# The closing stage of a two-layer macaron block: tail parts of the intermediate in products of 112 rows, turns at other tiles, squares summed on GpSimd, the HGRN result taken in halves

## The chip, the cores and the metric

The kernel runs on one core of a Trainium2 chip. A core has TensorE (PE; its weight loads, PEld, are shown apart), VectorE (DVE), ScalarE (ACT), GpSimd (POOL) and SyncE (SP), each with an instruction queue of its own, and 16 DMA engines. The metric is the time of one execution on the device, in microseconds (us). Of the kernel before there are three runs with a median of 2899.85 us.

## The reference, cut to what matters

The input is 16 sequences of 256 tokens with 256 features (4096 rows of 256). Two layers follow each other. The first (a mixture of experts, an attention, the same experts again) is not touched. The second is computed in the closing stage:

```python
    x = x + 0.5 * _L1_ffn_ref(_layernorm(x, axis=-1), L1_ffn_lut, L1_ffn_gate_idx, L1_ffn_up_idx, L1_ffn_down_idx)
    x = x + _L1_attn_ref(_layernorm(x, axis=-1), L1_attn_Wi, L1_attn_Wf, L1_attn_Wg, L1_attn_Wo, L1_attn_gnorm_w)
    x = x + 0.5 * _L1_ffn_ref(_layernorm(x, axis=-1), L1_ffn_lut, L1_ffn_gate_idx, L1_ffn_up_idx, L1_ffn_down_idx)
```

with, in `_L1_ffn_ref` (256 features, 688 in the intermediate, weights looked up in a table of 16 values),

```python
        gate = _ghost_linear(x, gate_idx, lut)
        up = _ghost_linear(x, up_idx, lut)
        h = jax.nn.silu(gate) * up
        return _ghost_linear(h, down_idx, lut)
```

and, in `_L1_attn_ref` (HGRN, a gated linear recurrence along the 256 tokens),

```python
        gate = jax.nn.sigmoid(f)
        v = jax.nn.silu(i) * (1.0 - gate)
        ...
        _, o = jax.lax.associative_scan(combine, (gate, v), axis=1)
        rms = o * jax.lax.rsqrt(jnp.mean(o * o, axis=-1, keepdims=True) + EPS)
        o = rms * gnorm_w * g * jax.nn.sigmoid(g)
        return jnp.einsum('btd,hd->bth', o, Wo)
```

## The kernel before, in words

The whole kernel is one launch with stages that follow each other: router, experts, attention, router, experts, and `closing`, which runs from about 2262 us to the end.

`closing` works on 8 units of 512 rows (four groups of 128, two sequences). A unit passes three stages: IN (first feed-forward), MID (HGRN) and OUT (second feed-forward). The loop over `i` goes through 10 rounds; round `i` has unit `i` in IN, `i-1` in MID and `i-2` in OUT, so rounds 2 to 7 have all three, round 0 only IN, round 1 IN and MID, round 8 MID and OUT, round 9 only OUT. The order on each engine is written out by hand in one block per engine, and semaphores join them; each engine works its list strictly in order.

TensorE's list in a full round (L1883 on): the six gate/up tiles of IN (`gate_up`, tiles 0 to 5), with the turn (transposition, `turn`) of unit `i-2` for OUT behind tile 1 and that of unit `i-1` for MID behind tile 3; the three HGRN projections f, i, g (`project`); `down` of IN; the turn of unit `i+1` for IN; the six gate/up tiles of OUT, with the sums of squares (`sums`) behind tile 3; `mix` (the product with the HGRN output weights); `down` of OUT. Products are made in three: each operand is split into a high and a low part, and high x high, high x low and low x high are added (`split_matmul`, L1433 to L1435).

The intermediate's 688 features are five tiles of 128 and a tail of 48 (tile 5). `UP_AT` is 64: a product of 112 columns makes the gate of the tail in rows 0 to 47 and its up part in rows 64 to 111 of one PSUM bank. ScalarE takes silu of the gate (`f_sil`, L1589), VectorE multiplies with up (`gated`, `f_hs`, L1680), ScalarE rounds the result to its high part (`high`, `f_hT`, L1594) and VectorE makes the low part (`low`, `f_hT`, L1686). `down` then does for each of four groups of 128 tokens 6 x 3 products, the last three of them over the 48 rows 64 to 111.

Banks: `pair[0]` and `pair[1]`, two banks each, are taken in turn by gate/up tiles and projections; `psT` (two banks) takes the turned tiles, which ScalarE reads as the high part (`f_lnT`, L1584) and VectorE as the low part (`f_lnT`, L1669); `psY` (two banks) takes `down` and `mix`. The sums of squares are written to four columns of `pair[1][0]`, from which VectorE makes `f_ms` (L1735) and GpSimd `f_orstd` (L1559). `mixed` (L1743) adds the HGRN result to the residual (`f_x`), for four groups in a row; moments (L1653, L1656), GpSimd's `norm` (L1539, L1541) and `normalise` (`f_ln`, L1663) prepare the next stage. GpSimd also adds the two halves of the input, `f_x` and `f_xb` (L1533).

## Time and profile before

| | us |
|---|---|
| median of 3 runs | 2899.85 (2894.0 to 2900.19) |
| the profiled execution | 2890.84 |
| its span, first to last instruction | 2889.1 |
| TensorE busy in it (mean granted clock 0.930) | 2472.3 (86%) |
| VectorE, ScalarE, GpSimd busy | 1782.9, 894.5, 1224.7 |

The page cuts the span into 40 slices of 72 us. The closing stage is the last nine of them. A digit is the busy share in tenths, and PEclk is the clock that TensorE was granted (9 is 90% or more of full speed):

```profile
PE   6455489999999999999999999956576489999997
PEld 5344378888888888888888888845454377777776
DVE  5332257787777777777777777745222266666543
ACT  6222223333333333333333333325322133333321
POOL 2277634545455545554555445421588221111110
PEclk9588889999999999999999999965789799999999
```

Two things in reading the order in time: a product's length is modelled to the end of its way through the array, so products overlap, and what counts is the distance from start to start; and "idle before" is counted from the modelled end of the instruction before.

### The profile page before, as it was taken

To read this page: it belongs to the slowest core of one execution; us is meant where nothing else is said; L and a number is where in the kernel's file an instruction comes from. 1 tells how busy PE (TensorE), PEld (TensorE's weight loads), DVE (VectorE), ACT (ScalarE), POOL (GpSimd) and SP (SyncE) were. 2 spreads that over 40 slices of the span, in tenths; PEclk is the share of its full clock that TensorE was granted. 3 is DMA by queue.
4 is the path that set the end of the run, shared out by engine and by line. 5 is a ranking of instruction groups with operands and counts; after the bars stand their busy time and mean duration, and the time that the engine had idled before them with its cause. 6 is when DMAs were issued, how large, how long until landed. Compare 5 with 4: busy or idle time off the path is not lost. (4 is left out here: it accounts for less than half of the span.)

```text
span 2889.1 us, 44938 instructions
## 1 busy us (share of the span) xinstructions
PE 2472.3 (86%) x17054; PEld 2122.6 (73%) x17054; DVE 1782.9 (62%) x3522; ACT 894.5 (31%) x1885; POOL 1224.7 (42%) x1193
## 2 busy tenths in 40 slices
PE   6455489999999999999999999956576489999997
PEld 5344378888888888888888888845454377777776
DVE  5332257787777777777777777745222266666543
ACT  6222223333333333333333333325322133333321
POOL 2277634545455545554555445421588221111110
PEclk9588889999999999999999999965789799999999
DMA  6699700000000000000000000014899210000000
GB/s 218 172 247 241 149 21 17 7 16 20 20 5 16 19 19 5 16 19 19 5 16 19 20 5 17 10 40 131 228 216 198 52 30 23 22 23 15 8 8 15
DMA packets 192917, 169.48 MB, mean 59 GB/s; under 512 B 28513, under 2 KB 185153, under 8 KB 192193
## 3 DMA queue, kind: packets, MB, share of 16 engines
q1 hardware_dynamic: 163472, 117.05, 13.7%
q0 software_dynamic: 24576, 37.77, 7.1%
q10 hardware_dynamic: 4656, 11.80, 1.3%
q8 instruction: 138, 2.26, 0.3%
q14 instruction: 75, 0.61, 0.1%
HBM read 117.88 MB, written 53.13 MB: 59 GB/s over the span
## 5 line engine op out<-in xcount | busy, mean ns | idle before, releaser
L947 POOL TENSOR_TENSOR a_orstd<-a_ms,minus_half 128x8 f32<-128x8 f32 x64 | 106.2, 1660 | 638.1 <-DVE a_ms L1107 638.1
L1080 DVE TENSOR_TENSOR a_at<-a_psB,causal 128x384 f32<-128x384 f32 x512 | 260.4, 550 | 101.6 <-PE a_psB L1252 101.6
L927 POOL TENSOR_SCALAR a_pick<-a_index,lut_row 128x258 f32<-128x258 int32 x240 | 278.9, 1162 | 24.4
L1100 DVE RECIPROCAL a_rz<-a_rz 128x256 f32<-128x256 f32 x128 | 221.5, 1732 | 0.0
L635 PE MATMUL e_psX<-ident,e_xg 128*128 128x128 f32 x256 | 62.7, 332 | 171.6 <-DMA e_xg<-rows,slot_tok 170.7
L759 DVE TENSOR_TENSOR e_hT<-e_psH,e_sil 128x128 f32<-128x128 f32 x128 | 37.3, 291 | 268.3 <-ACT e_sil L716 147.5
L635 PEld LDWEIGHTS e_psX<-ident,e_xg 128*128 128x128 f32 x256 | 32.6, 160 | 214.4 <-DMA e_xg<-rows,slot_tok 209.7
L930 POOL TENSOR_TENSOR a_found<-a_found,a_pick 128x258 f32<-128x258 f32 x240 | 177.5, 739 | 20.0
L1313 PE MATMUL a_psD<-a_v,a_at 128*128 128x128 f32 x1536 | 181.8, 275 | 0.0
L1313 PEld LDWEIGHTS a_psD<-a_v,a_at 128*128 128x128 f32 x1536 | 176.9, 192 | 0.1
L1680 DVE TENSOR_TENSOR f_hs<-f_pair,f_sil 128x512 f32<-128x512 f32 x96 | 66.2, 691 | 168.5 <-PE f_pair L1435 150.5
L606 POOL DMA_INDIRECT e_xg<-rows,slot_tok x128 | 128.0, 1000 | 91.1 <-POOLq L73 52.7
L1433 PE MATMUL f_pair<-f_lnT,wguT 128*128 128x512 f32 (+1 forms) x352 | 144.3, 410 | 18.2 <-DVE f_ms L1735 10.2
L1433 PE MATMUL a_psA<-wo_high,a_oT 128*128 128x256 f32 x512 | 151.9, 297 | 1.5 <-DVE a_oT L1060 1.5
L1028 ACT ACTIVATE a_sq<-a_psD 128x512 f32<-128x512 f32 x128 | 76.5, 598 | 240.5 <-PE a_psD L1313 227.7
L1434 PE MATMUL a_psA<-wo_low,a_oT 128*128 128x256 f32 x512 | 145.0, 283 | 0.0
L1435 PE MATMUL a_psA<-wo_high,a_oT 128*128 128x256 f32 x512 | 144.9, 283 | 0.0
L1435 PE MATMUL f_pair<-f_lnT,wguT 128*128 128x512 f32 (+1 forms) x352 | 140.2, 398 | 0.0
L1434 PE MATMUL f_pair<-f_lnT,wguT 128*128 128x512 f32 (+1 forms) x352 | 139.9, 397 | 0.0
L1589 ACT ACTIVATE f_sil<-f_pair 128x512 f32<-128x512 f32 x96 | 57.2, 597 | 260.4 <-PE f_pair L1435 260.4
L1433 PE MATMUL f_psY<-wdT,f_hT 128*128 128x256 f32 (+1 forms) x384 | 122.1, 318 | 14.5 <-DVE f_x L1743 7.6
L952 POOL TENSOR_TENSOR a_o<-a_o,a_orstd 128x512 f32<-128x512 f32 x128 | 131.0, 1044 | 5.0
(243 smaller groups left out, 7516.1 us busy)
## 6 DMA issues: line engine op xcount, KB each, us to landing
e_wg<-in_L_ffn_w_gate SPq DMA_DIRECT2D x128, 128.0 KB
e_wu<-in_L_ffn_w_up SPq DMA_DIRECT2D x128, 128.0 KB
e_wd<-in_L_ffn_w_down SPq DMA_DIRECT2D x128, 128.0 KB
rows<-r_row SPq DMA_DIRECT2D x32, 320.0 KB, 3.1
stream_b<-r_zeros SPq DMA_DIRECT2D x11, 384.0 KB, 6.2
stream_c<-rows SPq DMA_DIRECT2D x33, 128.0 KB, 3.2
r_xt<-in_L_attn_hidden_states SPq DMA_DIRECT2D x16, 256.0 KB, 3.9
stream_a<-r_xt SPq DMA_DIRECT2D x16, 256.0 KB, 4.9
```

The source lines that it names most:

```text
L606: pool.indirect_dma_start(out=xg[:, e % U, :], out_offset=None, in_=rows, in_offset=bass.IndirectOffsetOnAxis(ap=slot_tok[:, e:e + 1], axi ...
L635: nc.tensor.transpose(psX[u][:, c, :], xg[:, e % U, c * P:(c + 1) * P], cst["ident"][:, :]).then_inc(turned[u], 1)
L927: nc.gpsimd.tensor_scalar(pick[:, :, :], index[:, :, :], float(c), w["lut"][:, c:c + 1], ALU.is_equal, ALU.mult).then_inc(picked, 1)
L930: nc.gpsimd.tensor_tensor(out=found[:, :, :], in0=found[:, :, :], in1=pick[:, :, :], op=ALU.add).then_inc(looked, 1)
L947: nc.gpsimd.tensor_tensor(out=flat(orstd[:, :, :]), in0=ms[:, :], in1=cst["minus_half"][:, 0:TT * HQ], op=ALU.pow).then_inc(orstd_ok, 1)
L952: nc.gpsimd.tensor_tensor(out=part, in0=part, in1=orstd[:, :, 2 * a:2 * a + 2].unsqueeze(3).to_broadcast([P, TT, 2, DV]), op=ALU.mult).the ...
L1080: nc.vector.tensor_tensor(out=at[:, h, :], in0=psB[h % 2][:, 0:3 * P], in1=cst["causal"][:, :, :].rearrange("p a i -> p (a i)"), op=ALU.mu ...
L1100: nc.vector.reciprocal(rz[:, a, :], rz[:, a, :]).then_inc(rz_ok, 1)
L1313: mm = nc.tensor.matmul(psD[:, t, h * DV:(h + 1) * DV], bt[:, h, i * P:(i + 1) * P], v[:, n % 2, j, h * DV:(h + 1) * DV], start=(j == 0), ...
L1433: nc.tensor.matmul(out, lhs[0], rhs[0], start=first, stop=False)
L1434: nc.tensor.matmul(out, lhs[0], rhs[1], start=False, stop=False)
L1435: return nc.tensor.matmul(out, lhs[1], rhs[0], start=False, stop=last)
```

## The change

It touches `closing`, one weight group and one load of the expert stage before it.

1. The tail of the intermediate. `high` writes the tail's high part to rows 0 to 47 of `hT[:, 0, 5]`, `low` its low part to rows 64 to 111 of the same; rows 32 to 63 are zeroed once by ScalarE. The weights' tail lies in rows 0 to 47 and again in 64 to 111 (`down_groups`, and one more load of 64 columns). `down` makes two products of 112 rows for each group of tokens, against the weights' high and low part, where it made three of 48 rows (the product low x low comes with it). `down` also waits at its start for the low parts of the first five tiles alone, and for the tail's ahead of the first 112-row product.
2. The turns of OUT and MID come behind tiles 0 and 2 of IN, not 1 and 3; the moments of the next unit behind tile 3, not 4.
3. The squares of the two halves of features are added by GpSimd (`sum_of_squares`), the sums take 4 calls, not 8 (the trace has two records for a product of plain f32, so 16 for a unit before), and go to `psT[0]`, not `pair[1][0]`. The OUT tiles take the two pairs strictly in turn, and the last of them doesn't wait for `ms_ok`.
4. `mixed` is done in two halves, the low part of tile 5 between them, and `down` of OUT waits for each half apart.
5. The first unit's load comes in halves, and VectorE adds it (`add_first`), not GpSimd.

```diff
-    tail = [w_dn[:, c, INTER - UP_AT - FLAST:INTER] for c in range(DC)]
-    groups.append((wdT[UP_AT:UP_AT + FLAST, 0, FT - 1, :], wdT[UP_AT:UP_AT + FLAST, 1, FT - 1, :], tail, UP_AT))
+    tail = [w_dn[:, c, UPS:UPS + UP_AT + FLAST] for c in range(DC)]
+    groups.append((wdT[0:UP_AT + FLAST, 0, FT - 1, :], wdT[0:UP_AT + FLAST, 1, FT - 1, :], tail, 0))
...
-            return (f if stage == IN else 9 + f + (f >= 4)) % 2
+            return (f if stage == IN else 1 + f) % 2
...
+                def load_first():
+                    for k in range(2):
+                        half = slice(2 * k, 2 * k + 2)
+                        sp.dma_start(xb[:, half, :], sv[1][0][:, half, :]).then_inc(x_first[k], 16)
+                        sp.dma_start(x1[:, 0, half, :], sv[0][0][:, half, :]).then_inc(x_first[k], 16)
...
+                def sum_of_squares(m):
+                    pool.wait_ge(osq_ok, DC * m + DC)
+                    nc.gpsimd.tensor_tensor(out=osq[:, 0, :], in0=osq[:, 0, :], in1=osq[:, 1, :], op=ALU.add).then_inc(osum_ok, 1)
...
+                nc.scalar.activation(hT[32:UP_AT, 0, FT - 1, :].rearrange("p (g t) -> p g t", t=P),
+                                     cst["ident"][32:UP_AT, :].unsqueeze(1).to_broadcast([UP_AT - 32, G, P]), ACT.Copy,
+                                     scale=0.0).then_inc(tail_zero, 1)
...
-                        if f == 4 and i + 1 < U:
+                        if f == 3 and i + 1 < U:
                             moments_of(IN, i + 1)
...
+                    if mid is not None:
+                        mixed(mid, 0)
                     if last is not None:
                         low(OUT, last, FT - 1)
                     if mid is not None:
-                        mixed(mid)
+                        mixed(mid, 1)
...
-                def down(stage, m):
-                    pe.wait_ge(h_lo[stage], FT * m + FT)
-                    for k in range(2):
...
+                def down(stage, m, k):
+                    pe.wait_ge(h_lo[stage], FT * m + FT - 1)
+                    for g in (2 * k, 2 * k + 1):
+                        dst = psY[k][:, (g % 2) * D:(g % 2 + 1) * D]
+                        for f in range(FT - 1):
+                            split_matmul(nc, dst, [hT[:, part, f, g * P:(g + 1) * P] for part in range(2)],
+                                         [wdT[:, part, f, :] for part in range(2)], f == 0, False)
+                        if g == 0:
+                            pe.wait_ge(h_lo[stage], FT * m + FT)
+                            pe.wait_ge(tail_zero, 1)
+                        for part in range(2):
+                            mm = nc.tensor.matmul(dst, hT[0:UP_AT + FLAST, 0, FT - 1, g * P:(g + 1) * P],
+                                                  wdT[0:UP_AT + FLAST, part, FT - 1, :], start=False, stop=(part == 1))
+                    mm.then_inc(down_ps[stage], 1)
...
-                    pe.wait_ge(osq_ok, DC * m + DC)
+                    pe.wait_ge(osum_ok, m + 1)
+                    psT_free(m)
...
-                        if f == 1 and last is not None:
-                            turn(OUT, last)
-                        if f == 3 and mid is not None:
-                            turn(MID, mid)
+                        if f == 0 and last is not None:
+                            turn(OUT, last, mids)
+                        if f == 2 and mid is not None:
+                            turn(MID, mid, mids)
...
-                            pe.wait_ge(res_ok[MID], G * mid + G)
+                                pe.wait_ge(res_ok[MID], G * mid + 2 * k + 2)
```

`psT_free` makes TensorE wait until VectorE has read all earlier turned tiles (`lnT_lo`) and earlier sums (`ms_ok`).

How the lists move. VectorE in a full round, from the two results `f_y` of the unit that is done, through the IN tiles, before:

```order
L1700 SCALAR_TENSOR_TENSOR f_y<-f_psY,f_x 128x512 x2
L1680 TENSOR_TENSOR f_hs<-f_pair,f_sil 128x512
L1686 TENSOR_TENSOR f_hT<-f_hs,f_hT 128x512
L1680 TENSOR_TENSOR f_hs<-f_pair,f_sil 128x512
L1686 TENSOR_TENSOR f_hT<-f_hs,f_hT 128x512
L1669 TENSOR_TENSOR f_lnT<-f_psT,f_lnT 128x512 x2
L1680 TENSOR_TENSOR f_hs<-f_pair,f_sil 128x512
L1686 TENSOR_TENSOR f_hT<-f_hs,f_hT 128x512
L1680 TENSOR_TENSOR f_hs<-f_pair,f_sil 128x512
L1686 TENSOR_TENSOR f_hT<-f_hs,f_hT 128x512
L1669 TENSOR_TENSOR f_lnT<-f_psT,f_lnT 128x512 x2
L1653 BN_STATS f_bs<-f_x 128x6 x4
```

and with the change (L1669 became L1698, L1680 L1709, L1686 L1716, L1653 L1682):

```order
L1730 SCALAR_TENSOR_TENSOR f_y<-f_psY,f_x 128x512 x2
L1698 TENSOR_TENSOR f_lnT<-f_psT,f_lnT 128x512 x2
L1709 TENSOR_TENSOR f_hs<-f_pair,f_sil 128x512
L1716 TENSOR_TENSOR f_hT<-f_hs,f_hT 128x512
L1709 TENSOR_TENSOR f_hs<-f_pair,f_sil 128x512
L1716 TENSOR_TENSOR f_hT<-f_hs,f_hT 128x512
L1698 TENSOR_TENSOR f_lnT<-f_psT,f_lnT 128x512 x2
L1709 TENSOR_TENSOR f_hs<-f_pair,f_sil 128x512
L1716 TENSOR_TENSOR f_hT<-f_hs,f_hT 128x512
L1682 BN_STATS f_bs<-f_x 128x6 x4
L1685 BN_AGGR f_mv<-f_bs 128x2 x4
L1709 TENSOR_TENSOR f_hs<-f_pair,f_sil 128x512
```

The low parts of the turned tiles (`f_lnT`) stand right behind `f_y` and two gatings later, and the statistics (`f_bs`) one gating sooner.

VectorE at the end of a round, from `f_ms` to the statistics of the HGRN result, before:

```order
L1735 TENSOR_SCALAR f_ms<-f_pair 128x4
L1680 TENSOR_TENSOR f_hs<-f_pair,f_sil 48x512
L1686 TENSOR_TENSOR f_hT<-f_hs,f_hT 128x512
L1686 TENSOR_TENSOR f_hT<-f_hs,f_hT 48x512
L1743 SCALAR_TENSOR_TENSOR f_x<-f_psY,f_orstd,f_x 128x256 x4
L1653 BN_STATS f_bs<-f_x 128x6 x4
```

and with the change:

```order
L1765 TENSOR_SCALAR f_ms<-f_psT 128x4
L1709 TENSOR_TENSOR f_hs<-f_pair,f_sil 48x512
L1716 TENSOR_TENSOR f_hT<-f_hs,f_hT 128x512
L1773 SCALAR_TENSOR_TENSOR f_x<-f_psY,f_orstd,f_x 128x256 x2
L1716 TENSOR_TENSOR f_hT<-f_hs,f_hT 48x512
L1773 SCALAR_TENSOR_TENSOR f_x<-f_psY,f_orstd,f_x 128x256 x2
L1682 BN_STATS f_bs<-f_x 128x6 x4
```

The four `f_x` are now two and two, with the 48-row low part between them, and `f_ms` is read from `f_psT`.

TensorE in round 1, where there is no OUT unit: the turn for the next unit (into `f_psT`), the sums, `mix`, the first tile of round 2, before:

```order
L1811 MATMUL f_psT<-ident,f_ln 128x128 x8
L1850 MATMUL f_pair<-causal,f_osq 128x1 x8
L1859 MATMUL f_psY<-woT,f_pT 128x256 x8
L1433 MATMUL f_pair<-f_lnT,wguT 128x512
L1434 MATMUL f_pair<-f_lnT,wguT 128x512
```

and with the change:

```order
L1849 MATMUL f_psT<-ident,f_ln 128x128 x8
L1892 MATMUL f_psT<-causal,f_osq 128x1 x4
L1901 MATMUL f_psY<-woT,f_pT 128x256 x8
L1433 MATMUL f_pair<-f_lnT,wguT 128x512
L1434 MATMUL f_pair<-f_lnT,wguT 128x512
```

The sums are half as many and go to the bank into which the turn just ahead of them wrote.

## Rows read from the trace of the kernel before

**Rows 1.** Busy time by stage: start:end, us, each engine, clock, DMA share, GB/s.
```profile
2400.00:2793.00 393.00, 371.79 (x2026) 310.36 (x2026) 225.75 (x456) 115.58 (x202) 58.28 (x57) 1.00 0.06 17
2436.96:2508.43 71.47, 67.74 (x370) 56.50 (x369) 43.02 (x85) 21.71 (x38) 11.68 (x11) 1.00 0.07 23
```

**Rows 2.** Waits of TensorE, closing stage: waiter, releaser, total us, times, longest.
```profile
PE f_psT L1811 <- DVE f_ln L1663: 35.5, 2, 32.3
PE f_pair L1433 <- DVE f_lnT L1669: 17.3, 11, 2.9
PE f_pair L1433 <- DVE f_ms L1735: 10.2, 7, 1.5
PE f_psY L1433 <- DVE f_x L1743: 7.6, 7, 1.1
PE f_psY L1433 <- DVE f_hT L1686: 6.8, 2, 3.9
...
PE f_pair L1433 <- DVE f_hs L1680: 1.1, 2, 0.8
```

**Rows 3.** Order in time, TensorE, `down`: start, us, line, operation, [idle before].
```profile
2467.94 0.28 PE L1434 MATMUL f_psY<-wdT,f_hT 128*128 128x256 f32 x1
2468.06 0.28 PE L1435 MATMUL f_psY<-wdT,f_hT 128*128 128x256 f32 x1
2468.27 0.38 PE L1433 MATMUL f_psY<-wdT,f_hT 48*128 48x256 f32 x1
...
2468.81 0.39 PE L1433 MATMUL f_psY<-wdT,f_hT 128*128 128x256 f32 x1
2469.04 0.28 PE L1434 MATMUL f_psY<-wdT,f_hT 128*128 128x256 f32 x1
```

**Rows 4.** Order in time: first product of `down`, turn behind it, last `down`.
```profile
2463.86 0.28 PE L1433 MATMUL f_psY<-wdT,f_hT 128*128 128x256 f32 x1
...
2473.88 1.09 PE L1811 MATMUL f_psT<-ident,f_ln 128*128 128x128 f32 x8
...
2498.30 0.39 PE L1433 MATMUL f_psY<-wdT,f_hT 128*128 128x256 f32 x1 [1.09 <-DVE f_x L1743]
```

**Rows 5.** Order in time: a 128-column product and the 112-column one behind it.
```profile
2295.94 0.40 PE L1435 MATMUL f_pair<-f_lnT,wguT 128*128 128x512 f32 x1
2296.18 0.40 PE L1433 MATMUL f_pair<-f_lnT,wguT 128*112 128x512 f32 x1
```

**Rows 6.** Order in time: the one-column products.
```profile
2485.93 1.84 PE L1850 MATMUL f_pair<-causal,f_osq 128*128 128x1 f32 x16
```

**Rows 7.** Order in time, GpSimd: an addition in place.
```profile
2501.51 2.40 POOL L1533 TENSOR_TENSOR f_x<-f_x,f_xb 128x1024 f32<-128x1024 f32 x1
```

**Rows 8.** Order in time, TensorE: ahead of the HGRN projections.
```profile
2455.55 0.50 PE L1433 MATMUL f_pair<-f_lnT,whT 128*128 128x512 f32 x1 [1.19 <-DVE f_lnT L1669]
2455.88 0.39 PE L1434 MATMUL f_pair<-f_lnT,whT 128*128 128x512 f32 x1
```

**Rows 9.** Order in time, TensorE: the last gate/up tile.
```profile
2492.12 0.48 PE L1433 MATMUL f_pair<-f_lnT,wguT 128*112 128x512 f32 x1 [1.45 <-DVE f_ms L1735]
```

**Rows 10.** Order in time, VectorE: the two lows ahead of the last `down`.
```profile
2866.81 1.41 DVE L1686 TENSOR_TENSOR f_hT<-f_hs,f_hT 128x512 fp32r<-128x512 f32 x2
```

**Rows 11.** Order in time, all engines: first loads and first addition.
```profile
2263.03 0.50 SPq L1512 DMA_DIRECT2D f_x<-x_att  x1
...
2269.47 2.33 POOL L1533 TENSOR_TENSOR f_x<-f_x,f_xb 128x1024 f32<-128x1024 f32 x1 [15.68 <-DMA f_x<-x_att]
```

**Rows 12.** Order in time, VectorE in round 1.
```profile
2357.08 1.26 DVE L1669 TENSOR_TENSOR f_lnT<-f_psT,f_lnT 128x512 fp32r<-128x512 f32 x2
2358.64 1.38 DVE L1663 TENSOR_SCALAR f_ln<-f_x,f_mv,f_rstd 128x256 f32<-128x256 f32 x4 [0.30 <-POOL f_rstd L1541]
```

**Rows 13.** Order in time, TensorE: sums in round 1.
```profile
2355.44 1.84 PE L1850 MATMUL f_pair<-causal,f_osq 128*128 128x1 f32 x16
```

**Rows 14.** Order in time, VectorE: normalising beside GpSimd's addition.
```profile
2501.57 3.45 DVE L1663 TENSOR_SCALAR f_ln<-f_x,f_mv,f_rstd 128x256 f32<-128x256 f32 x4 [1.47 <-POOL f_rstd L1541]
```

More of the change, by code:

```diff
@@ L1801, in _, with psT_free @@
                 done_turns = [0, 0, 0]
-                def turn(stage, m):
-                    pe.wait_ge(ln_ok[stage], G * m + G)
+                def psT_free(sums):
                     for other in (IN, MID, OUT):
@@ L1807, in turn @@
                             pe.wait_ge(lnT_lo[other], DC * done_turns[other])
+                    if sums > 0:
+                        pe.wait_ge(ms_ok, sums)
+                def turn(stage, m, sums):
+                    pe.wait_ge(ln_ok[stage], G * m + G)
+                    psT_free(sums)
                     done_turns[stage] += 1
@@ L1861, in mix @@
                         mm.then_inc(out_ps, 1)
[L1863 removed]
+                turn(IN, 0, 0)
                 for i in range(U + 2):
@@ L1889, in _ @@
                             pe.wait_ge(res_ok[OUT], 2 * lasts)
-                        down(IN, first)
+                        for k in range(2):
+                            down(IN, first, k)
                     if i + 1 < U:
-                        turn(IN, i + 1)
+                        turn(IN, i + 1, mids)
                     for f in range(FT):
```

100 lines of the change are left out of this document (52 added, 48 removed).

## The prediction

> **What bounds the kernel now.** I read the page first (busy shares, the 40 slices), then the table by stage for the closing stage, then the waits of TensorE in it, then the order in time of each engine through one round. The diff touches the closing stage, from about 2262 us to the end, and one load and one weight group ahead of it. In that stage TensorE is the bound: between 2400 and 2793 us it is busy 371.79 of 393.00 us at a granted clock of 1.00 (2.4 GHz), VectorE 225.75, ScalarE 115.58, GpSimd 58.28 [rows 1]. One round, in which three units pass through their three stages, takes 71.47 us (2436.96 to 2508.43) and repeats, with VectorE busy 43.02 of it. So time goes only where TensorE's own list gets shorter, or where a wait in it goes. The waits of TensorE in the stage are short and few [rows 2]: 7 times `f_ms` (10.2 us), 7 times `f_x` (7.6), 11 times `f_lnT` ahead of a product (17.3), 2 times `f_hT` (6.8), 2 times `f_ln` (35.5, of which 32.3 is the start of the stage).
>
> **The change part by part.** All times are against the profiled execution, 2890.84 us with a span of 2889.1.
>
> *The tail of the intermediate.* A product group of `down` is 5 x 3 products of 128 rows and 3 of 48 rows. Starts of 128-row products lie 0.12 apart (2467.94, 2468.06) [rows 3]. Then the first 48-row one comes after 0.21, the next 128-row one 0.54 later (three products), and its successor after 0.23: 0.98 us for five steps that would take 0.60. So there are 0.38 us of pauses, about 0.19 for each of the two changes between 128 and 48 rows. A whole `down` takes 10.02 us in the first feed-forward (2463.86 to 2473.88) and 10.13 in the last (2498.30 to the end of the round at 2508.43) [rows 1, 4]. The change puts low under high in one operand of 112 rows and needs two products: 68 for a `down`. At 0.12 each, without the two pauses, that is 8.16 us, so 8 x 1.86 + 8 x 1.97 = 30.6 us less. Is a 112-row product followed and preceded by such a pause? No row of before has 112 rows. The nearest are, on one side, these 48-row ones, on the other the 112-column ones of `gate_up`, of which the first starts 0.24 behind a 128-column one of the same length, without a pause [rows 5]. If the pauses stay, only 64 products of 0.12 go: 7.7 us. I take 30.6, since the rows with a 112 beside a 128 are the nearer in size and show no pause, and keep 7.7 as the other end. A gain below 7.7 I exclude: products get fewer, none wider.
>
> The Trainium skill (TensorEngine Tiling (Array Packing), Key Properties), to be weighed against the pauses of 0.19 us in [rows 3] and their absence in [rows 5], says that a change of tiling mode drains TensorE, and its list of configurations has none between 64 rows and 128. By that rule a 112-row product stands in the same mode as its neighbours, and the sum is the 30.6; without the rule, by the 48-row rows alone, it would be 7.7. The trace agrees with the drain at 48 rows; no run of before shows 112.
>
> *The sum of squares.* 16 products of one column take 1.84 us to their modelled end, 1.68 of it before the next product can start [rows 5, 6]; 8 of them go, 0.84 us, for 8 units 6.7 us. The GpSimd addition stands for them: 128x1024 in place takes 2.40 us [rows 7], so half of it about 1.2. It starts when ScalarE's second square ends, some 3 us behind the scans and 16 ahead of the products, while GpSimd has nothing to do. So it costs nothing, except in the first round with a HGRN unit (below).
>
> *Turns sooner.* In each of 7 rounds TensorE waits before the HGRN projections for VectorE's second part of the turned tile, 1.19 us [rows 8]. The profile counts from the modelled end of the product before; without a wait the next starts 0.16 ahead of that end [rows 5], and behind a wait the second start comes after 0.33 us and not 0.23 (2455.55, 2455.88). So the wait is worth 1.19 + 0.26 = 1.45 us. The turn now comes one gate/up tile (12 x 0.23 = 2.78 us) earlier, and there is 2.78 + 1.39 of tiles behind it instead of 1.39. What is late next is the gating of tile 4, which the projections need as well and which the moments of the next unit now precede: gated 3 starts at the end of tile 3, and it, a low and the moments (0.7 + 0.6 + 1.85 us in this round) put gated 4 at +3.15 to +3.84, where TensorE needs it at about +4.0. So the wait goes, with 0.1 to spare. Saved: 7 x 1.45 = 10.2.
>
> *The sums in another bank.* TensorE's last tile of the output feed-forward waits for `f_ms`, 1.45 + 0.26 = 1.71 us [rows 9]. With the sums in `psT[0]` that tile waits only for a gating done long before. 7 x 1.71 = 12.0.
>
> *HGRN result by half.* Behind `mix` the last `down` waits for `f_x`, 1.09 + 0.26 = 1.35 us [rows 4]. Now VectorE does low 4, two of the four `f_x`, low 5, and the other two. Counted from the end of tile 4 at 0: tile 5 ends at 1.4, silu and gated 5 at 2.9, low 4 at 3.6, first two `f_x` at 4.4, low 5 at 5.1; `mix` ends at 5.0, its second half is taken by 5.95. `down` needs the first two at 5.0, low 5 at 6.8 and the others at 9.1. Nothing waits: 7 x 1.35 = 9.4. The three waits together: 31.6 us.
>
> *First `down` and last.* In round 0 and in the last one it waits 3.9 and 2.9 us for `f_hT` [rows 2]. Now it needs only the first of two lows at its start (0.7 of 1.41) [rows 10], in round 0 also without the moments before gated 5, which held it 1.0: 1.7 and 0.7. The 0.8 us that tile 4 of the last round waits for `f_hs` go too, since the tile uses the other pair [rows 2]. Together 3.2.
>
> *First unit's addition on VectorE.* GpSimd's 2.33 us [rows 11] become VectorE's second half, 0.7 by the nearest row (half of two 128x512 lows in 1.41) [rows 10]: 1.6 less. Two more DMA issues may move the landing by up to 0.9 (at most 0.50 each, as the issue at 2263.03 [rows 11]); bounds 0.7 and 1.6, I take 1.6, as the same bytes are moved. ScalarE's zeroing lies in its idle 35 us. The extra load of 64 KB in the expert stage is at most 0.3 us at 220 GB/s; I take 0.
>
> *What gets worse: rounds 1 and 2.* With no third unit in round 1, the sums follow straight on a turn, and now write where that turn's result still lies. VectorE has read it at 2357.08 + 1.26 = 2358.34, and the sums started at 2355.44 [rows 12, 13]. They then end near 2359.2, `mix` near 2362.9, the last `f_x` 0.9 later than before, and with it the normalising for which the turn of round 2 waits (35.5 - 32.3 = 3.2 us before [rows 2]). And that turn stands before tile 1 now: 2.8 us of products, which filled the wait before, come behind it. +3.7 us; the wait grows from 3.2 to about 5.
>
> Sum: -30.6 - 6.7 - 31.6 - 3.2 - 1.6 + 3.7 = -70.0 us. The profiled execution would be 2890.84 - 70.0 = 2820.8. The median of the runs lies 9.0 us above the profiled one, so there it is 2899.85 - 70.0 = 2829.9, say 2830.
>
> **The rivals.** *A, the pauses stay with 112 rows:* for it, that no row shows such a product; against, the rule and the 112-column rows. 30.6 becomes 7.7: 2853. *B, the projections keep waiting, for gated 4:* for it, the 0.1 of slack and VectorE's order; against, that VectorE's blocks are short. At most the whole 10.2 stays: 2840. *C, the turn of the output stage comes before its normalising is done, in every round:* it would end on the other side. In before, the normalising ends at 2501.57 + 3.45 = 2505.02 [rows 14], 11.4 after `mix` starts (its 3.6 us and the 1.09 end at 2498.30 [rows 4]); after, TensorE reaches the turn 3.6 + 8.2 + 2.8 = 14.3 or more after it, so 3 us are to spare, where before the turn had 5.8 more. Each us beyond the 3 costs 7 us; slower than before by more than the measurement tells it would be from 13.9 us of lateness on (70.0 / 7 = 10.0, 0.9 for the border of 0.2%, and the 3), at about 2906. Against it: VectorE is idle 28 of 71 us in a round. *D, GpSimd's new addition slows VectorE:* VectorE's normalising takes 1.38 us alone (2358.64) and 3.45 beside GpSimd's 2.40 us addition (2501.57) [rows 7, 12, 14], and the new addition falls on the two products `f_pT` right behind the scans. If they are held for all 1.2 us, VectorE comes to the result of `down` just as that now ends, and at most 1.2 x 7 = 8 us come back: 2838. The Trainium skill (GPSIMD Engine Reference, Specifications) says that GpSimd shares its SBUF interface with VectorE's operations of two SBUF inputs. The trace agrees in kind with the normalising, though that has one tensor input; with the rule the addition would slow just that pair.
>
> **How the numbers follow.** My case 0.70 (own range 2812 to 2838, which also has the 9 us between profiled and median runs), A 0.12, B 0.09, D 0.04, C 0.03, and 0.02 for a change that does not remove the waits at all (2830 + 31.6 = 2862). The range reaches down for that offset, and up to A: 2812 to 2854. A difference of 0.2% (6 us) is about what a measurement of this kernel tells from none. Faster by more than that in all but C: 0.95; within it 0.02; slower 0.03.
>
> **What would show it.** Right: one `down` at 8.2 us; starts at 0.12 through its 112-row products; 8 one-column products; rounds of 71.47 - 1.86 - 1.97 - 0.84 - 4.51 = 62.3 us; no TensorE wait for `f_ms`, `f_x` or, but for the two last rounds, `f_lnT`; one wait near 5 us for `f_ln` in round 2. Wrong: gaps around the 112-row products (A); waits for `f_hs` before the projections (B); waits for `f_ln` in every round (C); longer `f_pT` operations and waits before tiles 1 to 3 of the last feed-forward (D). The forecast fails as a whole if the clock in the middle is below 1.00.

## The result, and the profile after

| | before | after |
|---|---|---|
| median of 4 runs each, us | 2900.02 (2894.0 to 2902.39) | 2823.36 (2821.51 to 2824.11) |
| ratio, 95% interval | | 0.9735 [0.9723, 0.9747] |
| the profiled execution, us | 2890.84 | 2821.51 |
| closing stage, first turn to the end of the last product | 603.2 | 535.0 |
| a full round | 71.46 | 62.0 |

The change makes the kernel 2.65% faster. Profile against profile it is 69.3 us, and 68.2 of them lie between the first turn and the last product. The medians differ by 76.7, since the profiled execution of before lay 9 us under its median and that of after 2 under. The further 7 us are in no stretch of these two traces; the runs of before spread by 8. The traces of the changed kernel and of its variants below, whose code ahead of the closing stage is the same, reach the first turn anywhere between 2273.4 and 2283.2 us, so whole runs differ by up to 10 us before the stage begins. What a step is worth is therefore read from the stage and from the length of a round.

The page of the kernel after, its span, busy times and the two rows of TensorE in 40 slices (now of 70.5 us):

```profile
span 2819.7 us, 44733 instructions
PE 2424.1 (86%) x16926; PEld 2097.4 (74%) x16926; DVE 1792.7 (64%) x3524; ACT 895.8 (32%) x1886; POOL 1233.4 (44%) x1200
...
PE   6456569999999999999999999995465568999997
...
PEclk9988889999999999999999999995589979999999
```

TensorE has 128 records fewer: 64 are products of the tail, the other 64 are the two records of each of 32 sum calls. The busy time by stage, for just over six full rounds and for one of them, answers to [rows 1]:

```profile
2389.50:2766.00 376.50, 372.00 (x2104) 324.29 (x2103) 252.31 (x488) 129.27 (x225) 74.83 (x68) 1.00 0.06 19
2427.36:2489.33 61.97, 61.97 (x355) 54.15 (x353) 44.09 (x85) 21.83 (x38) 12.99 (x12) 1.00 0.09 26
```

In a round TensorE is busy for the whole 61.97 us at a clock of 1.00: no wait is left. VectorE works 44.09 us instead of 43.02, and still has 18 to spare. The waits of TensorE in the stage, which answer to [rows 2]:

```profile
PE f_psT L1849 <- DVE f_ln L1692: 35.0, 2, 29.7
PE f_pair L1433 <- DVE f_lnT L1698: 9.2, 4, 3.0
PE f_psY L1433 <- DVE f_hT L1716: 4.3, 2, 2.2
PE f_psT L1892 <- issue: 3.0, 1, 3.0
PE f_psT L1849 <- DVE f_lnT L1698: 2.2, 1, 2.2
```

`f_ms` and `f_x` are gone, and of the 11 waits for `f_lnT` ahead of a product 4 are left, all in rounds 0, 1, 8 and 9. `f_ln` stays at two: the start of the stage (32.3 became 29.7) and round 2, where 3.2 became 5.3. One is new, 3.0 us ahead of the sums of round 1 (L1892); it has no releaser in the profile ("issue"). TensorE's list there waits in `psT_free` for VectorE's read of the turned tile. The prediction's sign, no wait for `f_lnT` "but for the two last rounds", holds for rounds 2 to 7 alone: the two waits of round 0 and of the start of round 1 (2.2 and 3.0 us) were in before as well and were left out of it.

The tail in `down`, in the order in time of TensorE; this answers to [rows 3]:

```profile
2456.26 0.28 PE L1435 MATMUL f_psY<-wdT,f_hT 128*128 128x256 f32 x1
2456.38 0.40 PE L1880 MATMUL f_psY<-wdT,f_hT 112*128 112x256 f32 x2
2456.61 0.28 PE L1433 MATMUL f_psY<-wdT,f_hT 128*128 128x256 f32 x1
2456.74 0.28 PE L1434 MATMUL f_psY<-wdT,f_hT 128*128 128x256 f32 x1
```

The two 112-row products (one row of the trace, x2) start 0.12 behind their forerunner and take 0.23 together; the next 128-row one has no pause behind them either. And the projections start straight behind the last gate/up tile, where [rows 8] had 1.19 us:

```profile
2444.15 0.39 PE L1435 MATMUL f_pair<-f_lnT,wguT 128*112 128x512 f32 x1
2444.38 0.39 PE L1433 MATMUL f_pair<-f_lnT,whT 128*128 128x512 f32 x1
```

The next table sets the saving against the prediction's terms stretch by stretch, from the starts of the HGRN projections in the two traces (2336.17 and 2329.64 in round 1, 2384.10 and 2382.38 in round 2, 2741.41 and 2692.40 in round 7, 2800.61 and 2742.87 in round 8; ends at 2879.76 and 2810.06):

| stretch | terms of the prediction in it | forecast | measured |
|---|---|---|---|
| start to round 1 | 1.6 + 1.7 + 1.86 + 1.45 | -6.6 | -6.5 |
| round 1 to 2 | 1.86 + 0.84 + 1.45, less 3.7 | -0.5 | +4.8 |
| round 2 to 7 | 5 x 9.17 | -45.9 | -47.3 |
| round 7 to 8 | 3.83 + 0.84 + 1.71 + 1.35 | -7.7 | -8.7 |
| round 8 to the end | 3.94 + 0.84 + 1.71 + 1.35 + 0.7 + 0.8 | -9.3 | -12.0 |
| sum | | -70.0 | -69.7 |

The sum is right and its parts aren't: the second stretch is 5.3 us worse, and the others together are 5.0 better.

### The profile page after: what moved, and what is told of

Its sections match the earlier page's. It is cut to its first block and busy times, and to the rows that moved or that the text cites. A ratio compares the mean times of both kernels' runs of the same rounds, so it can differ in the third digit from the quotient of the medians.

```text
span 2819.7 us, 44733 instructions
## 1 busy us (share of the span) xinstructions
PE 2424.1 (86%) x16926; PEld 2097.4 (74%) x16926; DVE 1792.7 (64%) x3524; ACT 895.8 (32%) x1886; POOL 1233.4 (44%) x1200
## 5 line engine op out<-in xcount | busy, mean ns | idle before, releaser
L1080 DVE TENSOR_TENSOR a_at<-a_psB,causal 128x384 f32<-128x384 f32 x512 | 260.6, 551 | 100.7 <-PE a_psB L1252 100.7
L1709 DVE TENSOR_TENSOR f_hs<-f_pair,f_sil 128x512 f32<-128x512 f32 x96 | 66.1, 689 | 116.6 <-PE f_pair L1435 106.5
L700 ACT ACTIVATE e_xgT<-e_psX 128x256 f32<-128x256 f32 x128 | 49.0, 383 | 245.9 <-PE e_psX L635 245.3
L958 ACT ACTIVATE a_emT<-a_psC 128x512 f32<-128x512 f32 x64 | 38.3, 599 | 276.2 <-DVE a_rz L1096 276.2
```

Source lines behind the costliest of these rows:

```text
L1080: nc.vector.tensor_tensor(out=at[:, h, :], in0=psB[h % 2][:, 0:3 * P], in1=cst["causal"][:, :, :].rearrange("p a i -> p (a i)"), op=ALU.mu ...
```

## The experiments

All kernels are variants of after. In the tables "stage" is from the first turn to the end of the last product and "round" the length of a full round, both in the profiled execution; each median is set against runs of the kernel before that were made beside it, on the same chip. Their median was 2894.55 for the first four kernels (*e_tail3*, *e_rows48*, *e_third112*, *e_turns_back*), 2898.68 for the next three and 2892.75 for the last four.

### The tail: how many products, and what makes the pause

*e_tail3*: the three 48-row products in rows 64 to 111, as before, all else as after.

```diff
-                        for part in range(2):
-                            mm = nc.tensor.matmul(dst, hT[0:UP_AT + FLAST, 0, FT - 1, g * P:(g + 1) * P],
-                                                  wdT[0:UP_AT + FLAST, part, FT - 1, :], start=False, stop=(part == 1))
+                        n = rows_of(FT - 1)
+                        mm = split_matmul(nc, dst, [hT[n, part, FT - 1, g * P:(g + 1) * P] for part in range(2)],
+                                          [wdT[n, part, FT - 1, :] for part in range(2)], False, True)
```

> The changed kernel with its tail as in the kernel before: three products of 48 rows in rows 64 to 111, for each group of tokens. All else stays. Theory (the tail was worth 30.6 us: 64 products of 0.12 us and 128 pauses of 0.19): about 2823 + 31 = 2854 us, a down of 10.0 to 10.1 us again, starts 0.21 and 0.23 apart at the changes of rows. Rival (the tail gave only its products, and the other edits the rest): 2823 + 8 = 2831.

*e_rows48*: two products, but over rows 0 to 47 alone (the tail's low part is left out).

```diff
-                            mm = nc.tensor.matmul(dst, hT[0:UP_AT + FLAST, 0, FT - 1, g * P:(g + 1) * P],
-                                                  wdT[0:UP_AT + FLAST, part, FT - 1, :], start=False, stop=(part == 1))
+                            mm = nc.tensor.matmul(dst, hT[0:FLAST, 0, FT - 1, g * P:(g + 1) * P],
+                                                  wdT[0:FLAST, part, FT - 1, :], start=False, stop=(part == 1))
```

> The changed kernel with its two tail products over rows 0 to 47 alone, so the low part of the intermediate's tail is left out of the result. As many products as in the changed kernel, only fewer rows. Theory (a change between 128 and 48 rows makes a pause of 0.19 us): 64 x 0.38 = 24 us more, about 2847, and a down of 9.7 us. Rival (the pause came from the place at row 64 or from the third product, not from the number of rows): 2823, a down of 8.2.

*e_third112*: a third 112-row product (the one against the weights' low part is done twice).

```diff
-                        for part in range(2):
+                        for part, end in ((0, False), (1, False), (1, True)):
```

> The changed kernel with a third product of 112 rows in each group of tokens: the second is done twice, so the result has the product with the weights' low part twice. Theory (a product of 112 rows costs its 0.12 us and nothing else): 64 x 0.12 = 7.7 us more, about 2831, a down of 8.6. Rival (products of 112 rows cost more than others, which two of them hide): 15 us or more.

| | median (range), us | ratio [95%] | stage | round |
|---|---|---|---|---|
| e_tail3 | 2855.03 (2853.22 to 2857.25) | 0.9863 [0.9828, 0.9899] | 568.0 | 65.90 |
| e_rows48 | 2848.80 (2845.94 to 2853.23) | 0.9838 [0.9802, 0.9874] | 559.6 | 64.95 |
| e_third112 | 2836.86 (2829.16 to 2841.78) | 0.9798 [0.9758, 0.9838] | 541.4 | 62.97 |

With the old tail a round is 3.90 us longer, which over 8 units is 31 us, and the stage 33.0. With two products of 48 rows it is 2.95 longer, 0.37 for each of the 8 groups in a round; with a third product of 112 rows 0.97, 0.12 for each. So the old tail's 3.90 are one product more, 0.97, and 0.37 of pauses, 2.95, which add up.

By its median alone e_third112 would speak for its rival: it is 13.5 us above after's, and the theory had 7.7. Of the 14.6 us between the two profiled executions 8.1 lie ahead of the first turn (2283.2 against 2275.1), where the two kernels are the same, and 6.4 in the stage. The length of a round decides it: 0.97 more, not 1.9.

The order in time of TensorE in e_rows48 shows where the pauses are:

```profile
2472.08 0.28 PE L1435 MATMUL f_psY<-wdT,f_hT 128*128 128x256 f32 x1
2472.29 0.50 PE L1880 MATMUL f_psY<-wdT,f_hT 48*128 48x256 f32 x2
2472.72 0.38 PE L1433 MATMUL f_psY<-wdT,f_hT 128*128 128x256 f32 x1
2472.94 0.28 PE L1434 MATMUL f_psY<-wdT,f_hT 128*128 128x256 f32 x1
```

and beside it the same place in e_third112:

```profile
2462.21 0.28 PE L1435 MATMUL f_psY<-wdT,f_hT 128*128 128x256 f32 x1
2462.33 0.52 PE L1880 MATMUL f_psY<-wdT,f_hT 112*128 112x256 f32 x3
2462.69 0.28 PE L1433 MATMUL f_psY<-wdT,f_hT 128*128 128x256 f32 x1
```

0.21 ahead of the 48-row products and 0.43 + 0.22 behind, where 0.12, 0.24 and 0.12 would do; none around three of 112 rows (0.12, and 0.36 for the three). The 48 rows here lie at row 0 and before at row 64, and the pause is the same: it goes with the number of rows, not with their place or the number of products. Between 48 and 112 rows no run here tells where it begins. The Trainium skill (TensorEngine Tiling (Array Packing), Key Properties) says that a change of tiling mode drains TensorE, and lists none between 64 rows and 128. The runs agree: by that rule 112 rows is in the mode of its neighbours.

### The waits and the sums, one at a time

*e_turns_back*: the turns behind tiles 1 and 3, the moments at tile 4 again; ScalarE's and VectorE's reads of the turned tiles go back with them (not shown in the diff).

```diff
-                        if f == 0 and last is not None:
+                        if f == 1 and last is not None:
                             turn(OUT, last, mids)
-                        if f == 2 and mid is not None:
+                        if f == 3 and mid is not None:
                             turn(MID, mid, mids)
...
-                        if f == 3 and i + 1 < U:
+                        if f == 4 and i + 1 < U:
                             moments_of(IN, i + 1)
```

> The changed kernel with the turns of OUT and MID behind tiles 1 and 3 again, ScalarE's and VectorE's parts and the moments where they stood before. Theory: the wait for f_lnT ahead of the projections is back in 7 rounds, 7 x 1.45 = 10.2 us, and in round 2 tile 1 is done ahead of the turn again, 2.8 us less: about 7.4 more, 2831. Rival (the wait was given back elsewhere, or the early turn costs something in every round): 2823 or less.

*e_whole*: the tail's low part and then the HGRN result in one piece, for which `down` waits whole.

```diff
-                    if mid is not None:
-                        mixed(mid, 0)
                     if last is not None:
                         low(OUT, last, FT - 1)
                     if mid is not None:
+                        mixed(mid, 0)
                         mixed(mid, 1)
...
-                                pe.wait_ge(res_ok[MID], G * mid + 2 * k + 2)
+                                pe.wait_ge(res_ok[MID], G * mid + G)
```

> The changed kernel with the HGRN result taken whole: low 5 first, then all four f_x, and the last down waits for all of them. Theory: a wait of 1.1 us for f_x is back in 7 rounds, with what start and entry cost 1.35 each: 9.4 us more, about 2833. Rival (with f_ms no longer waited for, tile 5 is done sooner and VectorE is late by more, since it starts its f_x only behind silu, gating and two lows): the wait is longer than before, up to 2.5 us, 17 more, 2840.

*e_sums8*: eight sum calls for a unit, no addition on GpSimd.

```diff
-                        sum_of_squares(mid)
...
-                        mm = nc.tensor.matmul(psT[0][:, g:g + 1], osq[:, 0, g * P:(g + 1) * P], cst["causal"][:, 1, 0:1],
-                                              start=True, stop=True)
+                        for c in range(DC):
+                            mm = nc.tensor.matmul(psT[0][:, g:g + 1], osq[:, c, g * P:(g + 1) * P], cst["causal"][:, 1, 0:1],
+                                                  start=(c == 0), stop=(c == DC - 1))
```

> The changed kernel without GpSimd's addition of squares: 8 calls of one column (16 records) again, into the same bank. Theory: 8 x 0.89 = 7.1 us more, about 2830, less up to 1 us in round 1, where nothing changes in the wait for the turned tile. Rival (GpSimd's addition, beside which three f_pT records took 2.46 us instead of 1.41, costs time on the path): 5 us or less.

*e_bank*: the sums in `pair[1][0]`, the old order of pairs, and the last OUT tile waiting for `f_ms`.

```diff
-            return (f if stage == IN else 1 + f) % 2
+            return (f if stage == IN else 9 + f + (f >= 4)) % 2
...
-                    psT_free(m)
                     for g in range(G):
-                        mm = nc.tensor.matmul(psT[0][:, g:g + 1], osq[:, 0, g * P:(g + 1) * P], cst["causal"][:, 1, 0:1],
+                        mm = nc.tensor.matmul(pair[1][0][:, g:g + 1], osq[:, 0, g * P:(g + 1) * P], cst["causal"][:, 1, 0:1],
...
+                            if f == 5:
+                                if mid is not None:
+                                    pe.wait_ge(ms_ok, mid + 1)
```

> The changed kernel with the sums in pair[1][0] again, the pairs of the OUT tiles as before, and the waits for f_ms with them; GpSimd's addition stays. Theory: the wait for f_ms is back, 7 x 1.71 = 12.0 us, the waits of the last round for f_hs (1.0) too; but in round 1 the sums don't wait for the turned tile and mix isn't slow, 3.0 + 3.4 = 6.4 less, of which the wait of round 2 takes back what its chain (f_orstd, f_x, f_ln) decides. So +7 to +13: 2830 to 2836. Rival (the bank was without effect): 2823.

| | median (range), us | ratio [95%] | stage | round | round, against after |
|---|---|---|---|---|---|
| e_turns_back | 2835.84 (2826.26 to 2838.29) | 0.9787 [0.9747, 0.9826] | 548.5 | 63.71 | +1.71 |
| e_whole | 2832.77 (2826.84 to 2834.66) | 0.9770 [0.9747, 0.9793] | 545.8 | 63.37 | +1.37 |
| e_sums8 | 2830.87 (2827.54 to 2838.82) | 0.9777 [0.9750, 0.9804] | 543.9 | 62.90 | +0.90 |
| e_bank | 2834.72 (2829.56 to 2838.64) | 0.9778 [0.9753, 0.9802] | 546.7 | 63.89 | +1.89 |

Each brings back the wait it was to bring back, in the table of TensorE's waits of e_whole, of e_bank and of e_turns_back (one row of each):

```profile
PE f_psY L1433 <- DVE f_x L1773: 7.6, 7, 1.1
```

```profile
PE f_pair L1433 <- DVE f_ms L1765: 10.2, 7, 1.5
```

```profile
PE f_pair L1433 <- DVE f_lnT L1698: 17.5, 11, 3.0
```

Counts are those of [rows 2], and so are the totals, to 0.2 us. The forecast was 1.35, 1.71 and 1.45 in a round, the measured 1.37, 1.89 and 1.71. With the tail's 3.90 and the sums' 0.90 the five single steps add up to 9.77, against 9.46 for all at once: they are nearly independent of each other, and the round's saving is accounted for.

e_turns_back missed its expectation: its median is 2836 for 2831, and the stage is 13.5 us longer than in after, where 7.4 was said. Up to the projections of round 1 it loses 3.8 us (they start 58.4 us after the first turn instead of 54.6): the wait for `f_hT` in round 0 is 3.2 for 2.1, since the moments stand ahead of the last gatings again, the wait ahead of the projections is back, and the first `down` has 1.5 us of slow products, as it has in e_same (below), which is after itself. The last two rounds lose 3.0, of which 2.9 are slow products behind waits of 2.01 us that after has too. The edge between rounds 1 and 2 is 1.9 us shorter, 3.6 without the 1.7 of the wait that came back in it. In e_bank, whose sums don't wait for the turned tile, it is 5.4 shorter (its projections start 55.1 and 102.4 us after the first turn in rounds 1 and 2, those of after 54.6 and 107.3). So the bank has the larger share in the edge, and the order of the turns one too.

### The edge between rounds 1 and 2, and a faster version

After's trace shows the edge itself. TensorE in rounds 1 and 2, in order of time (the products of tile 0, from 2357.53 on, left out):

```profile
2349.97 1.84 PE L1892 MATMUL f_psT<-causal,f_osq 128*128 128x1 f32 x8 [2.98 <-issue]
2351.66 6.21 PE L1901 MATMUL f_psY<-woT,f_pT 128*128 128x256 f32 x16
...
2365.99 1.97 PE L1849 MATMUL f_psT<-ident,f_ln 128*128 128x128 f32 x8 [5.34 <-DVE f_ln L1692]
2367.61 0.77 PE L1433 MATMUL f_pair<-f_lnT,wguT 128*128 128x512 f32 x1
```

The 2.98 us are the forecast wait for the turned tile. What was not forecast is what follows: the eight records of the sums take 1.69 us and not 0.81 to the next start, and `mix` 5.87 (to the start of tile 0) and not 3.35. The granted clock of that stretch, beside the same work in e_fix3 (below), is 0.56 against 1.00 (2.4 GHz):

```profile
2351.70:2357.40 5.70, 5.70 (x16) 4.63 (x17) 1.04 (x3) 0.00 (x0) 1.01 (x1) 0.56 0.01 3
```

```profile
2346.00:2349.20 3.20, 3.20 (x16) 2.84 (x17) 3.04 (x12) 0.43 (x1) 1.02 (x1) 1.00 0.52 169
```

In these rows the time of the stretch comes first, then what each engine did in it, and the clock is the third number from the end. Most of 2351.7 to 2357.4 ran at the lower level, 1.2 GHz, after the 3 us in which TensorE did nothing. The last `f_x`, which needs `mix`, starts only at 2358.34, and the turn of round 2 hangs on it.

Three versions go against it, and after was run again beside them. *e_same* is after.

> The changed kernel itself, beside the next three. 2823 us by its earlier runs, up to 2832 by how far the kernel before moves from run to run.

*e_fix1*: the first unit's sums go to the old bank.

```diff
+        def ss_bank(m):
+            return pair[1][0] if m == 0 else psT[0]
...
-                    psT_free(m)
+                    if m > 0:
+                        psT_free(m)
+                    else:
+                        pe.wait_ge(ai_ok, DC)
...
+                    if i == 2:
+                        pe.wait_ge(ms_ok, 1)
```

> The changed kernel, but in round 1 the sums go to pair[1][0], which no tile uses then; all other rounds stay. Theory (in round 1 the sums wait 3.0 us for the turned tile's bank, TensorE then works at the low clock, and this moves mix, f_x and the turn of round 2 back by some 4.3): sums right behind the turn, mix at its 3.35 us, the turn of round 2 about 4.3 us sooner against the round's start, 4 us less in all. Rival (the turn of round 2 waits for f_ln by VectorE's own order, whatever the sums do): no change.

*e_fix2*: that, and the turn for OUT of round 2 behind tile 1.

```diff
-                        if f == 0 and last is not None:
+                        if f == (1 if i == 2 else 0) and last is not None:
                             turn(OUT, last, mids)
```

> As the one before, and in round 2 the turn of OUT stands behind tile 1 again; it stays behind tile 0 in all other rounds. Theory: another 2.8 us less, about 7 less than the changed kernel. Rival (the turn of MID two products later then waits for the first): nothing more.

*e_fix3*: both, and VectorE's and GpSimd's chain to that turn shortened in rounds 0 and 1 (GpSimd's part isn't shown in the diff); GpSimd's addition for the next unit comes behind VectorE's normalising in every round.

```diff
                     if i + 1 < U:
+                        if i >= 2:
+                            pool.wait_ge(ln_ok[OUT], G * (i - 1))
                         add(i + 1)
...
                         result(IN, first, 1)
+                        if i == 1:
+                            mean_square(mid)
+                        if i < 2:
+                            turned_low(IN, i + 1)
                         moments_of(MID, first)
-                    if i + 1 < U:
+                        if i == 1:
+                            mixed(mid, 0)
+                            mixed(mid, 1)
+                    if 2 <= i < U - 1:
                         turned_low(IN, i + 1)
```

> As the one before, and the chain to the turn of round 2 is made short: in round 1 VectorE does f_ms right behind the result of down and its f_x ahead of the normalising of the next unit, GpSimd f_orstd ahead of that unit's norm; in rounds 0 and 1 VectorE reads the turned tile ahead of the moments; GpSimd's addition of the next input waits until the OUT normalising is done, in every round. Theory: the wait of round 2 (5.3 us in the changed kernel) is gone but for 1 us, that after the turn in round 0 (3.0) shorter by 1.8, some 6 us less than the one before and 13 less than the changed kernel, about 2810. Rival (another step of the chain, the product with its low clock or the additions moved back, takes it over): 3 us less than the one before or fewer.

| | median (range), us | ratio [95%] | stage | projections of round 2, after the first turn |
|---|---|---|---|---|
| e_same | 2822.81 (2816.39 to 2827.50) | 0.9752 [0.9729, 0.9776] | 535.4 | 107.6 |
| e_fix1 | 2819.27 (2812.46 to 2820.88) | 0.9732 [0.9709, 0.9754] | 532.6 | 102.2 |
| e_fix2 | 2817.61 (2807.72 to 2823.78) | 0.9726 [0.9700, 0.9753] | 528.6 | 100.7 |
| e_fix3 | 2811.29 (2809.05 to 2814.27) | 0.9715 [0.9694, 0.9735] | 525.5 | 95.0 |

The same place in e_fix3, in order of time (the products of two tiles left out):

```profile
2345.14 0.95 PE L1911 MATMUL f_pair<-causal,f_osq 128*128 128x1 f32 x8
2345.95 3.70 PE L1920 MATMUL f_psY<-woT,f_pT 128*128 128x256 f32 x16
...
2356.71 1.09 PE L1865 MATMUL f_psT<-ident,f_ln 128*128 128x128 f32 x8 [1.50 <-DVE f_ln L1700]
```

e_fix1 takes 5.4 us out of the edge by the bank alone, with the turn left where it was: the wait for `f_ln` is then 6.3 us long but ends sooner. e_fix2 takes 1.5 more, where 2.8 was said: the tile that now comes ahead of the turn saves its 2.8, but the 12 products behind the turn take 4.9 us at starts 0.43 apart. e_fix3 takes another 5.7, as said, with 1.50 us of wait for `f_ln` left and 0.55 ahead of the next turn. It makes several changes at once, and which of them gives how much was not taken apart. The wait behind the turn in round 0 became 0.9 shorter, not 1.8, and one of 1.37 for `f_hs` came behind it. e_fix3 is the fastest version: its runs (2809.05 to 2814.27) lie under all of e_same's, 11.5 us lower in the median and 9.9 in the stage. e_fix1 and e_fix2 overlap with e_same in their runs; that they help rests on the profile.

e_fix1's stage is only 2.8 shorter than e_same's though its edge is 5.4 shorter. The rest is lost in rounds 8 and 9, where nothing was changed, after the same waits. TensorE in e_fix1 and in e_same at the projections of round 8:

```profile
2737.91 0.79 PE L1433 MATMUL f_pair<-f_lnT,whT 128*128 128x512 f32 x1 [2.01 <-DVE f_lnT L1701]
...
2743.19 0.52 PE L1433 MATMUL f_pair<-f_lnT,whT 128*128 128x512 f32 x1
```

```profile
2741.45 0.80 PE L1433 MATMUL f_pair<-f_lnT,whT 128*128 128x512 f32 x1 [2.01 <-DVE f_lnT L1698]
...
2744.18 0.61 PE L1433 MATMUL f_pair<-f_lnT,whT 128*128 128x512 f32 x1
```

Both begin with starts 0.43 apart (0.23 at full clock). In e_fix1 that lasts for 12 products, in e_same for 6, so 36 products take 11.0 us or 9.9. At the first tile of round 9, behind the same wait of 2.01 us, its 12 products take 4.45 us to the start of the next in e_fix1 and 2.87 in e_same. e_fix3 has both losses too, 2.8 us in all, so its edge is 12.6 us shorter than e_same's and its stage only 9.9.

The same happens at the first `down`. In e_same, the same kernel as after, it also begins behind a wait of 2.13 us:

```profile
2296.48 0.39 PE L1433 MATMUL f_psY<-wdT,f_hT 128*128 128x256 f32 x1 [2.13 <-DVE f_hT L1716]
...
2297.56 0.42 PE L1435 MATMUL f_psY<-wdT,f_hT 128*128 128x256 f32 x1
```

From 1.1 us after its start on, some 15 products start 0.21 apart, and the `down` takes 9.74 us, where after's takes 8.26. In exchange the gate/up tiles ahead of it are 1.4 us faster in e_same. Where the slow products fall thus differs from trace to trace of one and the same kernel.

## Why the prediction was right, point by point

**The time.** 2830 was said for the median and it is 2823.4; for the profiled pair the sum was -70.0 and is -69.3. The median lies in the stated range of 2812 to 2854. The 6.6 us between forecast and median are the offset of the profiled execution to the median, 9 us in before and only 2 in after; the forecast took the same 9 for both, without a cause. That the sum comes to within 0.7 us is in part luck, since the loss at rounds 1 and 2 met gains that were not in it either.

**The tail (-30.6).** Right. `down` takes 8.16 us in the first feed-forward (2452.54 to 2460.70) and 8.34 in the last, where 8.16 was said for both; e_tail3 is 3.90 a round slower, 31.2 for the 8 units. Product and pause were sized right (0.97 and 2.95 a round). The choice between the two ends, 112 rows beside 128 without a pause or 48 rows with one, is decided by e_rows48 and e_third112. Rival A is out.

**The sums (-6.7).** 0.90 a round, 7.2 in all. In round 1 they were a loss, since they brought the wait with them.

**The three waits (-31.6).** A round is 62.0 us, where 62.3 was said. Right in kind and somewhat small: 1.37, 1.89 and 1.71 measured for 1.35, 1.71 and 1.45. Rival B stood on 0.1 us of slack, and there was more. VectorE in one round of after, around the gating of tile 4:

```profile
2441.62 1.40 DVE L1682 BATCH_NORM_STATS2 f_bs<-f_x 128x6 f32<-128x256 f32 x4
2443.05 0.38 DVE L1685 BATCH_NORM_AGGREGATE f_mv<-f_bs 128x2 f32<-128x6 f32 x4
2443.35 0.66 DVE L1709 TENSOR_TENSOR f_hs<-f_pair,f_sil 128x512 f32<-128x512 f32 x1
```

Gated 4 ends at 2444.01, and the projections start at 2444.38, 0.37 later.

**First and last `down` (-3.2).** Right: the waits fell from 3.9 to 2.1 and from 2.9 to 2.2, and the one for `f_hs` went, 1.8 + 0.7 + 0.8.

**First addition (-1.6).** Too small. From the issue of the first load to the first turn there are 13.97 us in before (2262.61 to 2276.58) and 11.24 in after, 11.1 to 11.4 in every variant: 2.7 less. The last half of the load is there 5.8 us after the first issue (2263.82 to 2269.59), where the whole was there after 6.9 in before (2269.47). The first turn came only 1.5 us earlier, since after's first load was issued 1.2 later, which is within what the traces differ by.

**The clock, not in the sum.** In before the first 12 products of either `down` ran 0.21 apart (2868.72 to 2871.07), and in after, behind a wait of 2.1 or 2.2 us, they don't. The first two products of the last `down` in before, and in after:

```profile
2868.37 0.55 PE L1433 MATMUL f_psY<-wdT,f_hT 128*128 128x256 f32 x1 [2.94 <-DVE f_hT L1686]
2868.72 0.41 PE L1434 MATMUL f_psY<-wdT,f_hT 128*128 128x256 f32 x1
```

```profile
2801.68 0.36 PE L1433 MATMUL f_psY<-wdT,f_hT 128*128 128x256 f32 x1 [2.22 <-DVE f_hT L1716]
2801.87 0.28 PE L1434 MATMUL f_psY<-wdT,f_hT 128*128 128x256 f32 x1
```

That is about 1.3 us at either `down` (11.4 us before, where the others take 10.1), 1.2 at the projections of round 8 (11.1 us became 9.9) and 0.9 at the turn ahead of them (1.94 became 1.06). In round 0 the gate/up tiles lost 1.1 in the same way (60 products in 15.7 and then 16.8). Together 3.6 us; with the 1.4 that the five full rounds saved beyond their forecast it is the 5.0 by which the other stretches are better. The runs don't show that these 3.6 us are the change's doing: behind the same 2.13 us wait the first `down` takes 8.26 us in after and 9.74 in e_same, behind the same 2.22 us the last takes 8.38 in after and 9.88 in e_sums8, and rounds 8 and 9 of e_fix1, e_fix3 and e_turns_back are 2.8 to 3.0 us longer than after's behind the same waits.

**Rounds 1 and 2 (+3.7).** Mis-sized. The stretch was to be 0.5 shorter and is 4.8 longer, so the edge costs 9.0. The mechanism was named right (the sums in the bank of the turn, the turn of round 2 before tile 1); what failed is that the wait was priced at its own length. Of the 5.3 us, 3.4 are slow products right behind the 2.98 us (0.9 in the sums, 2.5 in `mix`). Another 0.8 is a slip in the sum: the +3.7 is worked out with the short sums, and the 6.7 us subtract the same 0.84 for that unit once more, though the wait for the turn swallows it. The turn, late by that, is itself followed by slow products: 24 in 7.1 us, where 6.5 were needed in before and 5.8 at full clock, so 0.5 more than before. The rest are small steps of the chain. The wait for `f_ln` that was forecast near 5 us is 5.3. e_fix1 shows the bank's share, 5.4.

**Rival C** (the turn of OUT too early in every round) is out: no wait for `f_ln` beyond round 2. The normalising ends 2.8 us ahead of the turn (2427.31 and 2430.14 in one round), where 3 were said to spare; the 14.3 in that sum is 14.6 by its own terms. It is the mechanism of round 2, though, where no third unit's products lie between.

**Rival D** (GpSimd's addition slows VectorE) exists and costs nothing. The two `f_pT` beside it in after:

```profile
2457.42 2.46 DVE L1760 SCALAR_TENSOR_TENSOR f_pT<-f_ag,f_nwh,f_o 128x512 f32<-128x512 f32 x2
```

with GpSimd at the same time:

```profile
2457.38 1.29 POOL L1570 TENSOR_TENSOR f_osq<-f_osq 128x512 f32<-128x512 f32 x1 [3.27 <-ACT f_osq L1628]
```

The pair takes 2.46 us and 1.41 in before (two records, not the three of e_sums8's expectation). VectorE then still waits 1.01 us for `down`'s second half. In e_sums8, which has no such addition, it takes 2 x 0.745 again, and the round is not shorter but longer by what its eight further records cost. The group of `f_pT` in e_sums8, busy time, mean ns of one (1165 in after) and idle before:

```profile
L1759 DVE SCALAR_TENSOR_TENSOR f_pT<-f_ag,f_nwh,f_o 128x512 f32<-128x512 f32 x14 | 9.8, 745 | 0.0
```

The pair loses 1.05 us, where the prediction had up to 1.2, and the slack behind it is 1 us more than the prediction gave it.

## What to carry to other kernels

Look at the number of rows of neighbouring products, not only at their count: a short operand stacked to 112 rows cost nothing beside 128-row products here, where one of 48 rows cost a pause on either side. Price a new wait of TensorE of two or three us with the products behind it at the lower clock, which can follow (3.4 us more behind 2.98 here) but need not, and look for it at the edges of a pipeline, where the units that used to lie between are missing. When waits repeat with a period, undo the parts one by one and compare the length of the period: it told 0.9 us apart, while whole runs moved by 10.

## What the runs showed of the hardware that was not expected

- A change between products of 128 and of 48 rows costs about 0.19 us each way at a spacing of 0.12, at rows 0 and at rows 64 alike; between 128 and 112 rows it costs nothing that these traces show.
- After 2.98 us without work, 5.7 us of products ran at a mean clock of 0.56. Shorter waits were followed by slow products in some traces and not in others, at the same place in the program: a wait of 2.13 us ahead of the first `down` (8.26 us in after, 9.74 in e_same, which is the same kernel), one of 2.22 us ahead of the last (8.38 in after, 9.88 in e_sums8), one of 2.01 us ahead of the projections of round 8 (behind one of 2.21 and 1.1 us of work; 6 slow products in e_same and 12 in e_fix1). So the length of a wait alone doesn't tell what follows it; what else decides was not settled.
- Two VectorE products of two tensor inputs took 2.46 us instead of 1.41 beside a GpSimd addition of 1.29 us, so they lost 1.05, most of the time that the two overlapped. The Trainium skill (GPSIMD Engine Reference, Specifications) says that the two engines share SBUF interfaces, with contention for VectorE operations in a 2-port perf mode or with two SBUF inputs; the trace agrees for the two inputs. The normalising, which has one tensor input, took 3.46 beside GpSimd's 2.40 us addition, and 1.38 once that was moved behind it; which mode it runs in no trace here shows. In after, and in e_fix3 in round 2:

```profile
2485.82 3.46 DVE L1692 TENSOR_SCALAR f_ln<-f_x,f_mv,f_rstd 128x256 f32<-128x256 f32 x4 [1.47 <-POOL f_rstd L1554]
```

```profile
2355.28 1.38 DVE L1700 TENSOR_SCALAR f_ln<-f_x,f_mv,f_rstd 128x256 f32<-128x256 f32 x4 [1.48 <-POOL f_rstd L1557]
```
